# State-space phase of a two-layer decoder: decay in PSUM, B rows by DMA, SBUF products on GpSimd

## What is computed

```
h  = w_in(norm(x)) + b_in                     norm over tokens and channels of a sequence
c  = conv3(h) + conv_b;  z = norm over tokens of c;  hs = silu(z);  gate = silu(h)
B, C = hs @ w_B + b_B, hs @ w_C + b_C         16 states each, per token
delta = softplus(hs @ (w_d1 w_d2) + b)        per channel and token
for each state n:  s_n[t] = exp(-n * delta[t]) * s_n[t-1] + delta[t] * hs[t] * B[t, n]
y  = sum_n s_n * C[:, n] + D * hs
x  = norm(2 x + norm(y * gate) @ w_out + b_out)      norms over channels
```

## Time and profile before

| | us |
|---|---|
| median of 3 runs (lowest, highest) | 3807.19 (3804.27, 3807.99) |
| profiled execution | 3807.05 |
| its span | 3805.3 |
| state-space phase: first scan to last scan | 69.4 to 876.3 |
| granted TensorE clock, mean of the span | 0.938 |

### The profile page before, as it was taken

The page is one execution under the profiler, slowest core; times in us unless marked ns, Lnnn a source line. Parts: engine busy times, 40 slices in busy tenths (PEclk is TensorE's granted clock), DMA queues, the critical chain, the costliest instruction groups (busy, mean ns, idle before and its releaser), DMA issues. The chain is left out here.

```text
span 3805.3 us, 48050 instructions
## 1 busy us (share of the span) xinstructions
PE 3331.1 (88%) x13206; PEld 1779.1 (47%) x13206; DVE 2103.4 (55%) x3459; ACT 2147.8 (56%) x4056; POOL 1113.1 (29%) x971
## 2 busy tenths in 40 slices
PE   3777787777999999998666999999999779999997
PEld 1222232224777777776222444444444444444443
DVE  3999999995666666665997333333434331111110
ACT  3566665664656565664555777777777442332332
POOL 2555544552222222211664333333333100000000
PEclk8888888888999999999987999999999989999999
DMA  3000000000000000000111000000000220000001
GB/s 163 9 17 17 17 14 17 11 14 17 16 20 15 20 15 20 15 18 22 42 44 46 10 12 17 12 17 12 15 14 12 78 94 14 22 17 19 22 17 58
DMA packets 63436, 99.94 MB, mean 26 GB/s; under 512 B 7168, under 2 KB 38032, under 8 KB 62864
## 3 DMA queue, kind: packets, MB, share of 16 engines
q1 hardware_dynamic: 63376, 99.23, 7.1%
HBM read 14.46 MB, written 4.19 MB: 5 GB/s over the span
## 5 line engine op out<-in xcount | busy, mean ns | idle before, releaser
L1274 POOL TENSOR_TENSOR d_pr<-d_pr,d_keep 128x512 f32<-128x512 f32 x256 | 320.1, 1271 | 567.0 <-ACT d_pr L1432 567.0
L235 PE MATMUL a_py<-a_prod,consts 128*128 128x512 f32 x512 | 342.9, 765 | 146.6 <-DVE a_prod L499 116.1
L217 POOL TENSOR_TENSOR a_bx<-a_bcopy,a_drive_u 128x512 f32<-128x512 f32 x256 | 347.6, 1361 | 355.3 <-ACT a_bcopy L406 314.5
L493 DVE TENSOR_TENSOR_SCAN a_state<-a_decay,a_bx 128x512 f32<-128x512 f32 x256 | 400.0, 1563 | 1.3 <-POOL a_bx L217 1.3
L688 POOL TENSOR_TENSOR b_pn<-b_e,b_inv 128x308 f32<-128x308 f32 x256 | 178.9, 699 | 695.8 <-DVE b_inv L852 694.0
L406 ACT ACTIVATE a_bcopy<-a_pb 128x512 f32<-128x512 f32 x256 | 151.0, 590 | 218.5 <-PE a_pb L249 203.8
L795 ACT ACTIVATE b_e<-b_e 128x308 f32<-128x308 f32 x256 | 117.7, 460 | 218.4 <-DVE b_e L861 218.2
L1827 PE MATMUL f_ph<-f_hb,wb 128*128 128x512 f32 x512 | 232.9, 599 | 6.3 <-ACT f_hb L1862 6.3
L235 PEld LDWEIGHTS a_py<-a_prod,consts 128*128 128x128 f32 x512 | 108.9, 235 | 266.4 <-DVE a_prod L499 184.6
L1827 PE MATMUL f_ph<-f_ha,wb 128*128 128x512 f32 x512 | 230.2, 598 | 2.3 <-DVE f_ha L1891 2.3
L1496 DVE TENSOR_SCALAR d_ln<-d_pn 128x512 f32<-128x512 f32 (+1 forms) x160 | 101.8, 636 | 197.8 <-PE d_pn L1327 197.8
(11 more groups left out here) (275 smaller groups left out, 7275.2 us busy)
## 6 DMA issues: line engine op xcount, KB each, us to landing
wb<-in_wb SPq DMA_DIRECT2D x1, 6714.0 KB, 33.6
x<-in_x SPq DMA_DIRECT2D x1, 4096.0 KB
a_xf<-x SPq DMA_DIRECT2D x16, 256.0 KB, 2.3
a_xt<-x SPq DMA_DIRECT2D x16, 256.0 KB, 2.3
x<-a_xo SPq DMA_DIRECT2D x16, 256.0 KB, 2.3
b_xf<-x SPq DMA_DIRECT2D x32, 128.0 KB, 2.0
b_xt<-x SPq DMA_DIRECT2D x32, 128.0 KB, 2.0
x<-b_xo SPq DMA_DIRECT2D x32, 128.0 KB, 2.0
```

The source lines that it names most:

```text
L217: gp.tensor_tensor(bx[:, k % 4, :], bcopy[:, k % 4, :], drive_u[:, p, :], ALU.mult).then_inc(*bxt.step("bx"))
L235: mm(py[:], S["ident"][:], prod[:, j % 4, :], start=j == 0, stop=j == SLOTS - 1).then_inc(*pey.step("y"))
L493: V.tensor_tensor_scan(state[:, j % 2, :], decay[:, j % 4, :], bx[:, j % 4, :], 0.0, ALU.mult, ALU.add).then_inc(*vs.step("scan"))
L1274: gp.tensor_tensor(half, half, keep[:].unsqueeze(1).to_broadcast([128, QP, SEQ]), ALU.mult).then_inc(*gmt.step(f"m{odd}"))
```

## The change

- `decay` moves from four SBUF buffers to two PSUM banks (those of pb). exp(r) now waits for scan(r-2).
- pb, its matmuls and bcopy's ACT copies go. ACT copies the 16 B rows of a group to SBUF (`row`), SP stores them to DRAM, and one DMA for each state spreads a row over the 128 partitions of bcopy, issued three slots ahead, behind bx(r-4).
- `cz`, `silu`, `gate`, `delta` and the tail's `gated` go from DVE to GpSimd. `norm` goes: ACT scales by rstd as it makes h, in four instructions of 128 columns.
- The front shifts by LEAD = 2 slots: front step k of group g+1 runs in slot k-2, steps 0 and 1 in slots 14 and 15 of the step before. Most front steps from the convolution on are numbered one higher, so they run one slot earlier than before. `sum` now stands behind the scan and product of slot 14.

```diff
+        def lead(stage, g, p, k, front):
+            if k < SLOTS - LEAD:
+                if front:
+                    stage(k + LEAD, g + 1, 1 - p)
+            elif not isinstance(g, int) or g + 2 < G:
+                stage(k + LEAD - SLOTS, g + 2, p)
...
+                def spread_row(g, p, k, first):
+                    if not first:
+                        sp.wait_ge(*bxt.at("bx", SLOTS * g + k - 4))
+                    sp.dma_start(bcopy[:, k % 4, :], S["rows"][p, k:k + 1, :].to_broadcast([128, N])
+                                 ).then_inc(spread[k % 4], 16)
...
+                        if main and k + 3 < SLOTS:
+                            spread_row(g, p, k + 3, not begun(g - 1) and k == 0)
...
+                        if front and k == 12:
+                            sp.wait_ge(*sf.at("row", g + 1))
+                            sp.dma_start(S["rows"][q], brow[:, q, :]).then_inc(stored_b, 16)
...
+                        if front and k >= 13:
+                            if k == 13:
+                                sp.wait_ge(stored_b, 16 * g + 32)
+                            spread_row(g + 1, q, k - 13, not begun(g))
...
-                            pool.wait_ge(*copy_t.at("b", r))
+                            pool.wait_ge(spread[k % 4], 16 * (4 * g + k // 4 + 1))
...
+                def front_pool(k, g, q):
+                    if k == 10:
+                        pool.wait_ge(*sf.at("crstd", g))
+                        gp.tensor_tensor(b4(zc[:]), b4(f1[:]), over(small[:, 7, :]), ALU.mult).then_inc(*gf.step("cz"))
+                    if k == 11:
+                        pool.wait_ge(*sf.at("sg1", g))
+                        gp.tensor_tensor(hs[:, q, :], zc[:], f1[:], ALU.mult).then_inc(*gf.step("silu"))
...
-                    if k == 11:
-                        pe.wait_ge(*vf.at("silu", g))
+                    if k == 12:
+                        pe.wait_ge(*gf.at("silu", g))
...
-                        A(h0, b4(pf[:]), ACT.Identity, bias=W["b_in"]).then_inc(*sf.step("h"))
-                    if k == 6:
+                        for b in range(NB):
+                            op = A(h0[:, b, :], b4(pf[:])[:, b, :], ACT.Identity, scale=small[:, 3, b:b + 1],
+                                   bias=W["b_in"])
+                        op.then_inc(*sf.step("h"))
+                    if k == 7:
...
+                        A(brow[:, q, :], pv[0:STATES, :], ACT.Identity, bias=W["b_bc"][0:STATES, :]
+                          ).then_inc(*sf.step("row"))
...
-                            A(bcopy[:, k % 4, :], pb[k % 2][:], ACT.Copy).then_inc(*copy_t.step("b"))
-                            if begun(r - 4):
-                                act.wait_ge(*vs.at("scan", r - 4))
-                            A(b4(d)[:, :, 1:SEQ], b4(delta[:, p, :])[:, :, 1:SEQ], ACT.Exp,
+                            if begun(r - 2):
+                                act.wait_ge(*vs.at("scan", r - 2))
+                            elif k < 2:
+                                act.wait_ge(*dzero.at(f"decay{k}", 0))
+                            A(b4(decay[k % 2][:])[:, :, 1:SEQ], b4(delta[:, p, :])[:, :, 1:SEQ], ACT.Exp,
...
-                            V.tensor_tensor_scan(state[:, j % 2, :], decay[:, j % 4, :], bx[:, j % 4, :],
+                            V.tensor_tensor_scan(state[:, j % 2, :], decay[j % 2][:], bx[:, j % 4, :],
```

More of the change, by code:

```diff
@@ L136, in ssm_phase @@
         store = ctx.enter_context(nc.semaphore("a_store"))
-        zero = tr("zero", "decay hpad")
-        vf = tr("vf", "sum sub ssum norm csum csub cssum cz clip silu gate relu delta")
-        sf = tr("sf", "sq lnv rstd h conv csq clnv crstd e1 ln1 sg1 e2 ln2 sg2 bc hi absz ez lz mid")
+        stored_b = ctx.enter_context(nc.semaphore("a_stored_b"))
+        spread = [ctx.enter_context(nc.semaphore(f"a_spread{i}")) for i in range(4)]
+        zero = tr("zero", "hpad")
+        dzero = tr("dzero", "decay0 decay1")
+        vf = tr("vf", "sum sub ssum csum csub cssum clip relu")
+        sf = tr("sf", "sq lnv rstd h conv csq clnv crstd e1 ln1 sg1 e2 ln2 sg2 row bc hi absz ez lz mid")
         pef = tr("pef", "mean var h conv bc z")
-        gf = tr("gf", "r1 lo u")
+        gf = tr("gf", "cz silu gate r1 lo delta u")
         exp_t = tr("exp", "decay")
-        copy_t = tr("copy", "b")
-        peb = tr("peb", "b")
         pec = tr("pec", "c")
@@ L150, in ssm_phase @@
         vs = tr("vs", "scan prod")
-        vt = tr("vt", "y gated norm out")
+        vt = tr("vt", "y norm out")
+        gt = tr("gt", "gated")
         st = tr("st", "sq ln rstd sq2 ln2 rstd2")
@@ L218, in step @@
                                              ALU.mult).then_inc(*bxt.step("bx"))
[L219 to L222, removed]
+                        if tail and k == 4:
+                            pool.wait_ge(*vt.at("y", g - 1))
+                            gp.tensor_tensor(t1[:], t1[:], gate[:, q, :], ALU.mult).then_inc(*gt.step("gated"))
+                        lead(front_pool, g, p, k, front)
+                for k in range(LEAD):
+                    front_pool(k, 0, 0)
                 drive(pool, G, step)
@@ L412, in step @@
                             tail_act(k, g - 1, 1 - p)
-                        if front:
-                            front_act(k, g + 1, 1 - p)
+                        lead(front_act, g, p, k, front)
+                for k in range(LEAD):
+                    front_act(k, 0, 0)
                 drive(act, G, step)
@@ L420, in _ @@
                 SC = V.scalar_tensor_tensor
+                for i in range(2):
+                    V.memset(decay[i][:], 0.0).then_inc(*dzero.step(f"decay{i}"))
                 def front_dve(k, g, q):
                     if k == 0:
+                        dve.wait_ge(load, 16 * g + 16)
+                        V.tensor_reduce(small[:, 0, :], b4(xf[:, q, :]), AX, ALU.add).then_inc(*vf.step("sum"))
+                    if k == 1:
                         dve.wait_ge(*pef.at("mean", g))
+                        if begun(g - 1):
+                            dve.wait_ge(*gf.at("silu", g - 1))
                         V.tensor_tensor(b4(f1[:]), b4(xf[:, q, :]), over(pf[:, 0:NB]), ALU.subtract
@@ L483, in step @@
                     for k in range(SLOTS):
-                        if front and k == 0:
-                            dve.wait_ge(load, 16 * g + 32)
-                            V.tensor_reduce(small[:, 0, :], b4(xf[:, 1 - p, :]), AX, ALU.add).then_inc(*vf.step("sum"))
                         if tail and k == 4:
@@ L502, in step @@
                             tail_dve(k, g - 1, 1 - p)
-                        if front:
-                            front_dve(k, g + 1, 1 - p)
+                        lead(front_dve, g, p, k, front)
+                for k in range(LEAD):
+                    front_dve(k, 0, 0)
                 drive(dve, G, step)
@@ L2011, in build @@
         W["b_bc"] = W["b_bc"][0:96, :]
+        S["rows"] = nc.dram_tensor("rows", (2, STATES, 4 * SEQ), F32, kind="Internal").ap()
         S["sel"] = sb("sel", [96, 32, 128], BF16)
```

135 lines of the change are left out of this document (63 added, 72 removed).

## The result

The changed kernel takes 3716.56 us (median of 4 runs, 3715.09 to 3717.99), the kernel before beside it 3807.59: ratio 0.9757, interval [0.9745, 0.9769]. That is 91 us saved. 127 were forecast (3680 us); the range, 3605 to 3735, holds the time.

The account below looks back on a forecast made before the run. DVE, 94% busy, bounds the first phase. 28.3 + 11.6 + 0.7 + 1.4 us, plus 0.7 for the clock, gave a 42.7 us period against 50.63; 127 us saved in all: 3680 us, range 3605 to 3735.

Parts of the forecast that it names:

- rival 3: Scan stays stretched beside GpSimd even with decay in PSUM; period 46.9 us, time 3751 us; chance 10%.
- rival 4: DMA broadcast of B rows lands late, making the kernel slower: about 3910 us at 13 us landing; chance 4%.
- Fixed slots: A group's preparation is a chain fixed to slots, which shorten from 3.2 to 2.3 us while it hardly does.
- leg 2: End of `cssum` to `relu`, paced by ACT: 11.6 us a group, DVE standing 3.4 us before `relu`.
- Rival 1: Preparation chain is hidden, DVE's waits vanish; period 36.6 to 38 us, time 3589 to 3610 us; chance 13%.
- clock share: PE at 1.2 GHz for a third of the phase adds 0.7 us a group, bounds 0 to 2.5.
- sq2 0.57: ACT's `sq2` in the stretch from `cssum` to `relu`, taken at 0.57 us without a wait.
- the C row behind the mean: DVE's product behind `sum` waits for its C row, held behind PE's mean matmul: 0.7 us a group.
- leg 1: Start of `relu` to end of the next `cssum`, paced by DVE: 28.3 us a group, C-row waits added separately.
- the convolution wait: DVE waits for a C row behind PE's convolution matmuls: 1.4 us a group, bounds 0 and 1.9.
- Rival 2: Low clock spreads, PE at 1.2 GHz most of a group; period 44.5 to 46 us, some 3718 us; chance 12%.

Follow-up runs that it names:

- The fillings: Three unused matmuls on PE before bc's wait for `silu`, against the changed kernel: 3689.5 us; with three more before the mean's wait for `sum`: 3671.92 us.

## Why the prediction was right, and where 36 us short

- **Decay in PSUM, right.** 1215 ns, at most 1224, against 1209; rival 3 (still stretched) is out, and decay in SBUF costs 138 us. The Trainium skill's extra 65 ns for a PSUM source (VectorE: DVE Perf Modes, TRN2 errata) isn't seen: 1214 on average against 1209 at best before, one SBUF source less.
- **Products on GpSimd, right.** 1.04 to 1.27 us each, always alike. Worth 65 us.
- **B rows by DMA, right.** 3.3 us to landing where 2.3 was taken. GpSimd waited for them 0.9 us in the whole phase, in two waits; rival 4 is out.
- **Fixed slots, chain of leg 2, right in kind.** Rival 1 (chain hidden, 3589 to 3610) is out: DVE stands before `relu`, 2.27 us where 3.4 was forecast, because 2.52 (3.66 in every other group) of the idle time comes one instruction earlier, at the C row behind bc and z. `clip`, at 1.42 in place of 0.34, lies in the same idle time; `csub` took 0.69, not 0.98.
- **The term that was mis-sized is the clock share.** The text had it that a group wholly at 1.2 GHz would cost 2.5 us, and took a third of it, 0.7, by the mean clock of 0.83. The fillings took away 46.0 - 43.2 = 2.8 us of a steady group on average, and 3.5 where the group then ran at about 42.5, more than the text's upper bound. The lower clock isn't spread evenly: it comes after PE stood, and what PE stood for is just what the chain wants next (bc behind `silu`, the mean behind `sum`). The bound of 2.5 was too low because z and y, which it didn't count, run at the lower clock too and stand ahead of `out`. The mean clock was no worse, 0.86.
- **Two terms of the sum were wrong with it.** "sq2 0.57" was taken as not waiting; it waited 1.69 and 2.82 by turns, since the out matmuls stand behind bc, z, y and pc. And the C row behind the mean waited 2.02, not 0.7. With PE filled the second is 0.58, so that term was right at the full clock and only mispriced at the lower one. The first is still 0.92: a link left out. At the full clock the sum was 42.0, and the filled kernel's better groups take 42.5: leg 2 is 0.9 over, by this link, and leg 1 is 0.4 under (30.0), by `csub` (0.3 shorter) and the convolution wait (1.16, not 1.4).
- **Luck: the first interval.** The sum took 15 equal periods from 15 equal ones of 50.63, which is a mean with a short first interval of 39.6 in it; a steady group took 51.4. The first interval of the changed kernel is 32.4, 10 us under 42.7. Had it been the forecast's 42.7, the time would have been some 3727 us: inside the range still, but 47 us off the forecast.
- **Rival 2** (12%, 3718 us) gave the measured time and the mean period (44.5 to 46) and named the mechanism, but with the sign of a mean clock under 0.7. It is local instead: a few instructions a group. The short first interval helps its number too.

The order and the clock each explain most of the same 3 us a group: moving three steps gave 63 us, one of them (`sum`) partly by the clock, and filling gave 45 without any move. How far they add wasn't tried.

## What to carry over

Where TensorE stands and then starts the link of a chain, look in the rows for the clock at which that link and the matmuls behind it run, and price them by it; the mean clock of the phase doesn't tell. Here stands of 3.3 and 3.7 us brought 1.2 GHz each time, and a stand of 2.0 us did in six groups of the filled kernel but not in the changed one. Take a steady period from intervals between groups, not from a mean with the first interval in it. When a critical chain crosses engines, read each engine's queue ahead of every link: here three moves of one or two slots, with no work removed, gave two thirds of what the whole change gave. With the products on GpSimd the scan with two SBUF sources made the kernel slower than before (3855 us), the scan with one made it 91 us faster, so price the two parts together.

## What the runs showed of the hardware that was not expected

- A DVE scan with two SBUF sources took 6.48 us for 1.21 of work and ended 1.1 us behind five GpSimd instructions in a row: it seems to have got no turn between them.
- A one-source DVE operation can be held too: `clip` took 1.42 us beside `bx` and 0.41 without; written with two sources 1.69 and 0.68. Either form is held by 1.0 us; the GpSimd product beside it had 1.1 us left when it started. The scans with one source in PSUM and one in SBUF, beside as many products, were not held at all (1224 ns at most).
- 2.7 us of useless matmuls in front of a wait made the kernel 27 us faster, since TensorE's next matmuls ran at 2.4 GHz (granted clock of the phase 0.91, and 0.96 with both fillings, where it was 0.86).
- The lower clock outlasts the stand: behind one of 3.3 us, PE was busy without a gap and `bc`, `z` and `y` together took 4.3 us in one group and 5.4 in the next; with the stand filled, 2.8.
